# Causal attention with 16 heads: every eighth zero-mask product is split between VectorE and GpSimd, with a ScalarE copy of the scores for GpSimd

## The chip, the cores and the metric

The kernel runs on one core of a Trainium2 chip. The metric is the device time of one execution in microseconds (us). The engines are TensorE (PE; its weight loads are listed as PEld), VectorE (DVE), ScalarE (ACT), GpSimd (POOL) and SyncE (SP). Each works through its own list of instructions in order, and they meet at semaphores.

## The reference

The whole reference is two transformer-like layers over 4096 tokens of width 256. The change touches only the attention of the first layer, with 16 heads of width 16:

```
q, k = rope(q), rope(k)                       # 16 heads, 4096 tokens, width 16
scores = einsum('bhsd,bhtd->bhst', q, k) / 4
scores = scores * tril(ones)
scores = where(scores == 0.0, -inf, scores)
out = einsum('bhst,bhtd->bhsd', softmax(scores), v)
```

A score that is exactly zero gets no weight, whether the causal mask made it so or not. So each exponential has to be multiplied by (score != 0).

## The kernel before

`phase_attend` works on transposed scores: 128 keys lie on the partitions and 512 queries on the free axis. The 16 heads form four groups g of HG = 4 heads. For each group the 4096 queries are cut into eight blocks j of BT = 512 (32 blocks in all). Block j runs over the key tiles kt = 0 .. 4j+3 of 128 keys. One (g, j, kt) is a step, and there are 576. The last four steps of a block meet the diagonal (`diag` = 0 .. 3) and work on the columns from `w0` on: 512, 384, 256 and 128 of them. All others have 512 columns. In the 448 steps off the diagonal `diag` is None.

A step has two units, pair 0 (heads 0 and 1) and pair 1 (heads 2 and 3). Unit u = 2n + pair, of step number n, uses the scores buffer u % 3 of `ps_s`: two PSUM banks, one for each head, three such buffers. A unit goes through three engines:

- TensorE, `score`, L795: two bf16 matmuls of 128x512 into `ps_s`. It first waits until VectorE has done unit u-3, which used the same buffer (semaphore `bank`).
- ScalarE, L847: one exponential of 128x1024 out of `ps_s` into `probs` in SBUF, which has four slots, one for each step.
- VectorE, L874: one `scalar_tensor_tensor` over 128x1024: (score != 0) times the exponential. Its first input is in PSUM, its second and its output are in SBUF.

In diagonal steps GpSimd then cuts the triangle with one `affine_select` over four heads of 128x128 (L887). At last TensorE does `weigh` (L808): for each of the four heads a f32 matmul with the values, which accumulates in `ps_o` (each is listed as two instructions, so eight in a step).

The order on TensorE is written out by hand: for step n it is score(n, pair 1), score(n+1, pair 0), weigh(n-2). So an odd unit (pair 1) is always scored behind a `weigh`, and an even unit right behind an odd one. Once a block, ScalarE also copies the 128x512 result of the block before out of PSUM (L838, in the second diagonal step for j > 0). The key and query transfers are issued by SyncE.

Of the kernel before, what the change touches and what calls it, by code (L numbers as in the profile page):

```python
# [9 lines left out]
ALU = mybir.AluOpType  # L10
ACT = mybir.ActivationFunctionType
# [11 lines left out]
BT = 512  # L23
NB = T // BT
TT = BT // P
NT = T // P
HG = 4
# [91 lines left out]
class Carver:  # L119


    def __init__(self, tensor, at=0):
        self.tensor, self.at = tensor, at
        self.size = tensor.shape[1]
# [509 lines left out]
class Step:  # L634


    def __init__(self, n, g, j, kt):
        self.n, self.g, self.j, self.kt = n, g, j, kt
        self.block = g * NB + j
        self.slot = n % 4  # L640
        self.first = kt == 0
        self.diag = kt - TT * j if kt >= TT * j else None
        self.last = self.diag == TT - 1
        self.w0 = P * self.diag if self.diag else 0

    def unit(self, pair):

        return 2 * self.n + pair

    def masked(self):  # L650

        return self.block * TT + self.diag + 1
# [8 lines left out]
def all_steps():  # L661

    n = 0
    for g in range(NG):
        for j in range(NB):
            for kt in range(TT * (j + 1)):
                yield Step(n, g, j, kt)
                n += 1
# [5 lines left out]
def copied_in(step):  # L674


    if step.diag == (1 if step.j else 2) and step.block:
        return step.block - 1
# [18 lines left out]
def phase_attend(nc, m):  # L697


    with ExitStack() as ctx:  # L700
        own = []

        def sem(name):
            own.append(nc.alloc_semaphore(name="b_" + name))
            return own[-1]
# [4 lines left out]
        a = Carver(m.arena2)  # L710
        probs = a.take(4, HG, BT)
        a = Carver(m.arena, HG * T)
        q_stack = a.take(2, HG, BT, dt=BF16)
        o_raw = a.take(BT)
        recips = a.take(TT, HG)
        o_out = a.take(2, TT, HG, DH)

        ps_s = pb("ps_s", [P, 3, 2, BT])
        ps_o = pb("ps_o", [P, 2, BT])

        scored, exped, bank, probs_free = sem("scored"), sem("exped"), sem("bank_free"), sem("probs_free")
        masked, kload, o_copied = sem("masked"), sem("k_loaded"), sem("o_copied")
        o_turned, o_ready, recip_done = sem("o_turned"), sem("o_ready"), sem("recip_done")
        q_in = [sem("q_in0"), sem("q_in1")]
        o_stored = [sem("o_stored0"), sem("o_stored1")]
        block = ctx.enter_context(nc.Block())
# [52 lines left out]
        @block.tensor  # L779
        def _(pe):  # L780
            pe.wait_ge(m.kload_first, 16 * 8 * (NB - 1))

            def score(step, pair):
                u = step.unit(pair)
                if step.first and pair == 0:
                    pe.wait_ge(q_in[step.block % 2], 128 * (step.block // 2 + 1))
                    if step.block == NB - 1:
                        pe.wait_ge(m.kload_last, 128)
                    if step.j == 0 and step.g > 0:
                        pe.wait_ge(kload, 128 * step.g)  # L790
                if u >= 3:
                    pe.wait_ge(bank, u - 2)
                for h in range(2):
                    head = step.g % 2 * HG + 2 * pair + h
                    last = pe.matmul(ps_s[:, u % 3, h, step.w0:], m.k_stack[:, head, step.kt * P:step.kt * P + P],  # L795
                                     q_stack[:, step.block % 2, 2 * pair + h, step.w0:], start=True, stop=True)
                last.then_inc(scored, 1)

            def weigh(step):
                if step.first and step.block >= 2:  # L800
                    pe.wait_ge(o_ready, step.block - 1)
                if step.diag is None:
                    pe.wait_ge(bank, step.unit(1) + 1)
                else:
                    pe.wait_ge(masked, step.masked())
                for h in range(HG):
                    at = (step.kt * NH + step.g * HG + h) * (DH + 1)
                    last = pe.matmul(ps_o[32 * h:32 * h + 32, step.block % 2, step.w0:], m.values_flat[:, at:at + 32],  # L808
                                     probs[:, step.slot, h, step.w0:], start=step.first, stop=step.last,
                                     tile_position=(0, 32 * h))  # L810
                last.then_inc(probs_free, 1)

            def turn_over(b):
                pe.wait_ge(o_copied, b + 1)
                for t in range(TT):
                    last = pe.transpose(ps_o[:, b % 2, t * P:t * P + P], o_raw[:, t * P:t * P + P], m.ident[:])
                last.then_inc(o_turned, 1)

            with pe.If(bounded(pe) > 0):
                steps = list(all_steps())  # L820
                score(steps[0], 0)
                for step in steps:
                    score(step, 1)
                    if step.n + 1 < len(steps):
                        score(steps[step.n + 1], 0)
                    if step.n >= 2:
                        weigh(steps[step.n - 2])
                    if turned_in(step) is not None:
                        turn_over(turned_in(step))
                weigh(steps[-2])  # L830
                weigh(steps[-1])
                turn_over(BLOCKS - 1)

        @block.scalar
        def _(act):
            def copy_out(b):
                act.wait_ge(probs_free, steps_through(b))
                act.activation(o_raw, ps_o[:, b % 2], ACT.Copy).then_inc(o_copied, 1)  # L838

            with act.If(bounded(act) > 0):  # L840
                for step in all_steps():
                    if step.n >= 4:
                        act.wait_ge(probs_free, step.n - 3)
                    for pair in range(2):
                        u = step.unit(pair)
                        act.wait_ge(scored, u + 1)
                        act.activation(probs[:, step.slot, 2 * pair:2 * pair + 2, step.w0:], ps_s[:, u % 3, :, step.w0:], ACT.Exp,  # L847
                                       scale=1.0 / DH ** 0.5).then_inc(exped, 1)
                    if copied_in(step) is not None:
                        copy_out(copied_in(step))  # L850
                copy_out(BLOCKS - 1)

        @block.vector
        def _(dve):
            def normalise(b):
                dve.wait_ge(o_turned, b + 1)
                turned = ps_o[:, b % 2].rearrange("p (a c) -> p a c", a=TT * HG)
                if b >= 1:
                    dve.wait_ge(o_ready, b)
                dve.reciprocal(recips.rearrange("p t h -> p (t h)"), turned[:, :, DH]).then_inc(recip_done, 1)  # L860
                dve.wait_ge(recip_done, b + 1)
                if b >= 2:
                    dve.wait_ge(o_stored[b % 2], 64 * (b // 2))
                dve.tensor_tensor(o_out[:, b % 2].rearrange("p t h d -> p (t h) d"), turned[:, :, 0:DH],
                                  recips.rearrange("p t (h a) -> p (t h) a", a=1).to_broadcast([P, TT * HG, DH]), ALU.mult)\
                   .then_inc(o_ready, 1)

            with dve.If(bounded(dve) > 0):
                for step in all_steps():
                    for pair in range(2):  # L870
                        u = step.unit(pair)
                        dve.wait_ge(exped, u + 1)
                        p = probs[:, step.slot, 2 * pair:2 * pair + 2, step.w0:]
                        dve.scalar_tensor_tensor(p, ps_s[:, u % 3, :, step.w0:], 0.0, p, ALU.not_equal, ALU.mult).then_inc(bank, 1)  # L874
                    if normalised_in(step) is not None:
                        normalise(normalised_in(step))
                normalise(BLOCKS - 1)

        @block.gpsimd
        def _(pool):  # L880
            with pool.If(bounded(pool) > 0):
                for step in all_steps():
                    if step.diag is not None:

                        pool.wait_ge(bank, step.unit(1) + 1)
                        sq = probs[:, step.slot, :, step.w0:step.w0 + P]
                        pool.affine_select(out=sq, in_=sq, compare_op=ALU.is_ge, fill=0.0, base=0,  # L887
                                           pattern=[[0, HG], [1, P]], channel_multiplier=-1).then_inc(masked, 1)
# [1164 lines left out]
```

## Time and profile before

| | |
|---|---|
| median of three runs | 2300.75 us (2298.0 to 2304.64) |
| the profiled execution | 2298.0 us, of which the span from first to last instruction is 2296.3 us |
| busy over the span | PE 88%, DVE 75%, ACT 60%, POOL 24% |
| mean granted TensorE clock | 0.970 of full speed, 1.00 in most of the attention stage |
| attention stage | from about 189 us to about 1463 us of the span |

Times on the timeline are microseconds from the start of the span. An instruction's row gives its start and its duration. On ScalarE and VectorE the next instruction may begin some 0.1 us before the one ahead of it has ended, so the distance from start to start is what an instruction really takes of its engine when it stands in a queue. The count after x says how many instructions a row merges. A text in square brackets is the idle time ahead of the instruction and what ended it. "Releaser" is the profile's own inference.

### The profile page before, as it was taken

Reading aid. Unit: us, or ns where it says so; the run is one execution under the profiler, and the core shown is the slowest. Engines: PE = TensorE matmul, PEld = TensorE weight load, DVE = VectorE, ACT = ScalarE, POOL = GpSimd, SP = SyncE. Lnnn points to the kernel's source line nnn. Section 1 sums busy time; section 2 is a strip of 40 time slices with the busy share of each in tenths; the row PEclk is TensorE's granted clock in tenths of the full one; section 3 lists DMA queues with packets and bytes.
Section 4 is the critical chain, followed back from the end, with each engine's and each line's share of the span. In section 5 each row is a group of like instructions: output and inputs, shape, how many; then the busy total and the mean of one; then the engine's idle time right before and its main releaser. Section 6 shows DMA issues by size and latency. Waiting matters only on the chain. (4 is left out here: it accounts for less than half of the span.)

```text
span 2296.3 us, 28755 instructions
## 1 busy us (share of the span) xinstructions
PE 2009.7 (88%) x10349; PEld 807.0 (35%) x10349; DVE 1714.2 (75%) x2280; ACT 1366.9 (60%) x1729; POOL 542.7 (24%) x553
## 2 busy tenths in 40 slices
PE   4986999998999989999989999589886699999997
PEld 3541111111111121111121111256654356777775
DVE  2776999999999999999999999557665543333332
ACT  0675888888888888888888888345554211111110
POOL 1681000000000010000010000026655174323324
PEclk8997999999999999999999999899998899999999
DMA  3463211102111111212530000210000043444441
GB/s 110 155 197 96 42 30 22 30 14 52 21 31 22 30 45 35 38 21 64 163 102 12 13 12 3 80 37 20 18 1 1 7 148 115 113 103 93 110 102 23
DMA packets 124641, 133.85 MB, mean 58 GB/s; under 512 B 35145, under 2 KB 118946, under 8 KB 123808
## 3 DMA queue, kind: packets, MB, share of 16 engines
q1 hardware_dynamic: 109920, 118.09, 19.0%
q0 software_dynamic: 14592, 14.08, 3.5%
q8 instruction: 76, 1.25, 0.2%
q14 instruction: 53, 0.43, 0.1%
HBM read 97.08 MB, written 50.63 MB: 64 GB/s over the span
## 5 line engine op out<-in xcount | busy, mean ns | idle before, releaser
L874 DVE SCALAR_TENSOR_TENSOR arena<-ps_s,arena 128x1024 f32<-128x1024 f32 (+3 forms) x1152 | 1212.7, 1128 | 49.8 <-ACT arena L847 43.5
L847 ACT ACTIVATE arena<-ps_s 128x1024 f32<-128x1024 f32 (+3 forms) x1152 | 1046.0, 952 | 226.1 <-PE ps_s L795 221.5
L795 PE MATMUL ps_s<-arena 128*128 128x512 bf16 (+3 forms) x2304 | 648.0, 368 | 119.0 <-DVE arena L874 56.1
L808 PE MATMUL ps_o<-arena,values 128*32 128x512 f32 (+3 forms) x4608 | 574.8, 571 | 0.4 <-POOL arena L887 0.4
L795 PEld LDWEIGHTS ps_s<-arena 128*128 128x128 bf16 x2304 | 136.3, 97 | 792.7 <-DVE arena L874 770.0
L887 POOL TENSOR_SCALAR_AFFINE_SELECT arena<-arena 128x512 f32<-128x512 f32 x128 | 81.6, 637 | 1201.8 <-DVE arena L874 1201.8
L1801 ACT ACTIVATE arena<-g_ps_g 128x320 f32<-128x320 f32 (+1 forms) x96 | 42.2, 439 | 310.8 <-PE g_ps_u L1735 310.8
L1986 POOL DMA_INDIRECT out<-values,slot_ids x80 | 123.4, 1543 | 240.6 <-DVE values L1950 212.3
L1923 DVE TENSOR_TENSOR arena<-g_ps_u,arena 128x320 f32<-128x320 f32 (+1 forms) x96 | 47.2, 492 | 168.3 <-ACT arena L1801 168.3
L808 PEld LDWEIGHTS ps_o<-arena,values 128*32 128x32 f32 x4608 | 90.8, 108 | 225.3 <-issue 207.7
L1228 PE MATMUL t_ps_out<-arena 128*128 128x256 f32 x512 | 124.8, 402 | 19.7 <-DVE arena L1458 8.8
L1735 PE MATMUL g_ps_g<-arena 128*128 128x320 f32 (+1 forms) x384 | 119.7, 434 | 0.6 <-issue 0.6
L1735 PE MATMUL g_ps_u<-arena 128*128 128x320 f32 (+1 forms) x384 | 120.1, 435 | 0.0
L1228 PEld LDWEIGHTS t_ps_out<-arena 128*128 128x128 f32 x512 | 102.3, 203 | 42.3 <-issue 19.9
L1750 PE MATMUL g_ps_d<-arena 128*128 128x256 f32 (+1 forms) x480 | 107.9, 381 | 1.0 <-DVE arena L1923 1.0
L1750 PEld LDWEIGHTS g_ps_d<-arena 128*128 128x128 f32 (+1 forms) x480 | 89.5, 189 | 15.2 <-DVE arena L1923 1.6
L1967 POOL DMA_INDIRECT slots_in_dram<-arena,scatter_at x64 | 70.3, 1099 | 55.0 <-issue 55.0
L1236 PE MATMUL t_ps_turn<-ident,arena 128*128 128x128 f32 x256 | 37.4, 294 | 51.1 <-ACT arena L1122 18.8
L1950 DVE SCALAR_TENSOR_TENSOR values<-g_ps_d,arena,gates 128x256 f32<-128x256 f32 x80 | 35.8, 481 | 61.9 <-PE g_ps_d L1750 61.9
L1735 PEld LDWEIGHTS g_ps_u<-arena 128*128 128x128 f32 (+1 forms) x384 | 69.8, 182 | 34.5 <-issue 0.6
L1735 PEld LDWEIGHTS g_ps_g<-arena 128*128 128x128 f32 (+1 forms) x384 | 69.5, 181 | 33.2 <-issue 1.4
L1325 ACT ACTIVATE arena<-t_ps_turn,mod_cols 128x512 f32<-128x512 f32 x48 | 34.8, 775 | 71.5 <-PE t_ps_turn L1236 71.5
(198 smaller groups left out, 1640.2 us busy)
## 6 DMA issues: line engine op xcount, KB each, us to landing
arena<-parts_dram SPq DMA_DIRECT2D x320, 64.0 KB, 2.3
parts_dram<-arena SPq DMA_DIRECT2D x32, 384.0 KB, 2.9
arena<-parts_dram SPq DMA_DIRECT2D x24, 512.0 KB, 7.0
slots_in_dram<-in_empty_slots SPq DMA_DIRECT2D x10, 1040.0 KB, 25.8
arena<-slots_in_dram SPq DMA_DIRECT2D x16, 650.0 KB, 4.6
arena<-in_L_ffn_w_gate SPq DMA_DIRECT2D x16, 352.0 KB, 3.1
arena<-in_L_ffn_w_up SPq DMA_DIRECT2D x16, 352.0 KB, 3.8
arena<-in_L_attn_x SPq DMA_DIRECT2D x8, 512.0 KB, 3.9
```

Of the source, the lines that this page charges most:

```text
L795: last = pe.matmul(ps_s[:, u % 3, h, step.w0:], m.k_stack[:, head, step.kt * P:step.kt * P + P], q_stack[:, step.block % 2, 2 * pair + h, ...
L808: last = pe.matmul(ps_o[32 * h:32 * h + 32, step.block % 2, step.w0:], m.values_flat[:, at:at + 32], probs[:, step.slot, h, step.w0:], sta ...
L847: act.activation(probs[:, step.slot, 2 * pair:2 * pair + 2, step.w0:], ps_s[:, u % 3, :, step.w0:], ACT.Exp, scale=1.0 / DH ** 0.5).then_i ...
L874: dve.scalar_tensor_tensor(p, ps_s[:, u % 3, :, step.w0:], 0.0, p, ALU.not_equal, ALU.mult).then_inc(bank, 1)
L887: pool.affine_select(out=sq, in_=sq, compare_op=ALU.is_ge, fill=0.0, base=0, pattern=[[0, HG], [1, P]], channel_multiplier=-1).then_inc(ma ...
L1228: last = pe.matmul(ps_out[:, c, t * D:t * D + D], lhs[:, k, at:at + P], w[:, k], start=k == 0, stop=k == KC - 1)
L1735: last = pe.matmul(ps[0:rows_, n % 2, 0:HALF], w[:, s, k, at:at + rows_], inT[:, s, k, half * HALF:half * HALF + HALF], start=k == 0, stop ...
L1750: last = pe.matmul(ps_d[:, (s + i) % 2, at:at + D], hidden_e[0:rows_, s, f, c * P:c * P + P], w_down[0:rows_, s, f], start=f == 0, stop=f ...
L1801: act.activation(silu_e[0:rows_, n % 2], ps_g[0:rows_, n % 2, 0:HALF], ACT.Silu).then_inc(silued, 1)
L1923: dve.tensor_tensor(hidden_e[0:rows_, s, i, half * HALF:half * HALF + HALF], ps_u[0:rows_, n % 2, 0:HALF], silu_e[0:rows_, n % 2], ALU.mul ...
L1967: pool.indirect_dma_start(out=m.slots_in[:, :], out_offset=bass.IndirectOffsetOnAxis(ap=m.scatter_at[:, k, t:t + 1], axis=0), in_=m.h_wide ...
L1986: pool.indirect_dma_start(out=out_rows, out_offset=bass.IndirectOffsetOnAxis(ap=ids[:, s, c:c + 1], axis=0), in_=rows_out[:, s, c], in_off ...
```

## The change

In every step with `diag` None and kt % 4 == 1 (kt = 1, 5, 9, ... 4j-3; j of them in block j, 28 for each group, 112 in all) the last head's product leaves VectorE. VectorE's instruction of pair 1 then covers one head (128x512). ScalarE copies the last head's 128x512 scores out of `ps_s` into `s_copy` in SBUF, behind the exponential of pair 1. GpSimd turns the copy into ones and zeros with a `tensor_scalar`, and multiplies the exponentials by it with a `tensor_tensor`. TensorE waits for the copy (`scores_out`) before it scores pair 0 two steps later (kt % 4 == 3), which uses the same buffer, and for GpSimd's product (`last_masked`) before it weighs the step.

```diff
+        self.shared = self.diag is None and kt % 4 == 1
...
+        return self.g * NB * (NB - 1) // 2 + self.j * (self.j - 1) // 2 + min((self.kt + 2) // 4, self.j)
...
+        s_copy = a.take(BT)
...
                 if u >= 3:
                     pe.wait_ge(bank, u - 2)
+                if pair == 0 and step.kt % 4 == 3 and step.diag is None:
+                    pe.wait_ge(scores_out, step.shares())
...
                 if step.diag is None:
                     pe.wait_ge(bank, step.unit(1) + 1)
+                    if step.shared:
+                        pe.wait_ge(last_masked, step.shares() + 1)
...
+                    if step.shared:
+                        if step.shares():
+                            act.wait_ge(last_masked, step.shares())
+                        act.activation(s_copy, ps_s[:, step.unit(1) % 3, 1], ACT.Copy).then_inc(scores_out, 1)
...
-                        p = probs[:, step.slot, 2 * pair:2 * pair + 2, step.w0:]
-                        dve.scalar_tensor_tensor(p, ps_s[:, u % 3, :, step.w0:], 0.0, p, ALU.not_equal, ALU.mult).then_inc(bank, 1)
+
+                        heads = 1 if step.shared and pair == 1 else 2
+                        p = probs[:, step.slot, 2 * pair:2 * pair + heads, step.w0:]
+                        dve.scalar_tensor_tensor(p, ps_s[:, u % 3, 0:heads, step.w0:], 0.0, p, ALU.not_equal, ALU.mult).then_inc(bank, 1)
...
+                    if step.shared:
+                        pool.wait_ge(scores_out, step.shares() + 1)
+                        pool.wait_ge(exped, step.unit(1) + 1)
+                        pool.tensor_scalar(s_copy, s_copy, 0.0, 0.0, ALU.is_equal, ALU.is_equal).then_inc(kept, 1)
+                        pool.wait_ge(kept, step.shares() + 1)
+                        p = probs[:, step.slot, HG - 1]
+                        pool.tensor_tensor(p, p, s_copy, ALU.mult).then_inc(last_masked, 1)
```

## Rows read from the trace of the kernel before

**Rows 1.** The attention stage: busy us (xcount) of each engine, granted clock, DMA.

```profile
185.00:1465.00 1280.00, 1163.94 (x7040) 239.57 (x7040) 1231.42 (x1216) 1058.17 (x1184) 81.56 (x128) 0.99 0.18 39
```

**Rows 2.** The page's costliest groups: busy us, mean ns, idle before, releaser.

```profile
L874 DVE SCALAR_TENSOR_TENSOR arena<-ps_s,arena 128x1024 f32<-128x1024 f32 (+3 forms) x1152 | 1212.7, 1128 | 49.8 <-ACT arena L847 43.5
L847 ACT ACTIVATE arena<-ps_s 128x1024 f32<-128x1024 f32 (+3 forms) x1152 | 1046.0, 952 | 226.1 <-PE ps_s L795 221.5
...
L887 POOL TENSOR_SCALAR_AFFINE_SELECT arena<-arena 128x512 f32<-128x512 f32 x128 | 81.6, 637 | 1201.8 <-DVE arena L874 1201.8
```

**Rows 3.** VectorE's masking by shape, all of the span.

```profile
L874 DVE SCALAR_TENSOR_TENSOR arena<-ps_s,arena 128x1024 f32<-128x1024 f32 x960 | 1092.3, 1217 | 22.4 <-ACT arena L847 19.2
...
L874 DVE SCALAR_TENSOR_TENSOR arena<-ps_s,arena 128x512 f32<-128x512 f32 x64 | 43.6, 686 | 3.1
```

**Rows 4.** Timeline of ACT, DVE, PEld around kt = 5 of one block (start, us).

```profile
924.91 1.02 ACT L847 ACTIVATE arena<-ps_s 128x1024 f32<-128x1024 f32 x1 [0.32 <-PE ps_s L795]
...
925.83 1.02 ACT L847 ACTIVATE arena<-ps_s 128x1024 f32<-128x1024 f32 x1
...
927.17 1.02 ACT L847 ACTIVATE arena<-ps_s 128x1024 f32<-128x1024 f32 x1 [0.33 <-PE ps_s L795]
...
925.99 1.22 DVE L874 SCALAR_TENSOR_TENSOR arena<-ps_s,arena 128x1024 f32<-128x1024 f32 x1
...
927.12 1.22 DVE L874 SCALAR_TENSOR_TENSOR arena<-ps_s,arena 128x1024 f32<-128x1024 f32 x1
...
926.52 0.11 PEld L795 LDWEIGHTS ps_s<-arena 128*128 128x128 bf16 x2 [0.84 <-DVE arena L874]
927.25 0.11 PEld L795 LDWEIGHTS ps_s<-arena 128*128 128x128 bf16 x2 [0.62 <-DVE arena L874]
927.79 0.16 PEld L808 LDWEIGHTS ps_o<-arena,values 128*32 128x32 f32 x8 [0.42 <-issue]
928.79 0.11 PEld L795 LDWEIGHTS ps_s<-arena 128*128 128x128 bf16 x2 [0.84 <-DVE arena L874]
```

**Rows 5.** Timeline around kt = 1 of the same block.

```profile
914.53 1.93 ACT L847 ACTIVATE arena<-ps_s 128x1024 f32<-128x1024 f32 x2
...
916.65 1.02 ACT L847 ACTIVATE arena<-ps_s 128x1024 f32<-128x1024 f32 x1 [0.18 <-PE ps_s L795]
...
917.72 1.02 ACT L847 ACTIVATE arena<-ps_s 128x1024 f32<-128x1024 f32 x1
...
916.94 1.22 DVE L874 SCALAR_TENSOR_TENSOR arena<-ps_s,arena 128x1024 f32<-128x1024 f32 x1
...
918.07 1.22 DVE L874 SCALAR_TENSOR_TENSOR arena<-ps_s,arena 128x1024 f32<-128x1024 f32 x1
```

**Rows 6.** Timeline of ACT, its copy out of PSUM and the next exponential.

```profile
908.52 0.59 ACT L838 ACTIVATE arena<-ps_o 128x512 f32<-128x512 f32 x1
...
909.00 0.60 ACT L847 ACTIVATE arena<-ps_s 128x512 f32<-128x512 f32 x1
```

**Rows 7.** Timeline where VectorE waited for an exponential.

```profile
912.35 1.02 ACT L847 ACTIVATE arena<-ps_s 128x1024 f32<-128x1024 f32 x1
...
913.40 1.23 DVE L874 SCALAR_TENSOR_TENSOR arena<-ps_s,arena 128x1024 f32<-128x1024 f32 x1
```

**Rows 8.** A GpSimd product with two SBUF inputs: duration ns min/median/max.

```profile
L516 POOL TENSOR_TENSOR arena<-arena x32: 1146/1160/1608, 67.0 to 173.9; 128x512 f32<-128x512 f32 x32
```

**Rows 9.** VectorE lines, some beside GpSimd: duration ns min/median/max, first and last start.

```profile
L471 DVE TENSOR_TENSOR arena<-arena x32: 679/1020/1662, 65.4 to 171.3; 128x512 f32<-128x512 f32 x32
...
L458 DVE TENSOR_TENSOR arena<-ps_p,arena x16: 658/692/693, 62.9 to 167.2; 128x512 f32<-128x512 f32 x16
...
L874 DVE SCALAR_TENSOR_TENSOR arena<-ps_s,arena x1152: 414/1215/1226, 191.5 to 1459.4; 128x1024 f32<-128x1024 f32 x160, 128x768 f32<-128x768 f32 x20, 128x256 f32<-128x256 f32 x12
```

**Rows 10.** Timeline at kt = 1 of a block j = 1.

```profile
837.00 1.03 ACT L847 ACTIVATE arena<-ps_s 128x1024 f32<-128x1024 f32 x1
...
839.13 1.22 DVE L874 SCALAR_TENSOR_TENSOR arena<-ps_s,arena 128x1024 f32<-128x1024 f32 x1
```

More of the change, by code:

```diff
@@ L644, in __init__, with shares @@
         self.w0 = P * self.diag if self.diag else 0
+        self.shared = self.diag is None and kt % 4 == 1
     def unit(self, pair):
         return 2 * self.n + pair
+    def shares(self):
+        return self.g * NB * (NB - 1) // 2 + self.j * (self.j - 1) // 2 + min((self.kt + 2) // 4, self.j)
     def masked(self):
@@ L723, in phase_attend @@
         o_turned, o_ready, recip_done = sem("o_turned"), sem("o_ready"), sem("recip_done")
+        scores_out, kept, last_masked = sem("scores_out"), sem("kept"), sem("last_masked")
         q_in = [sem("q_in0"), sem("q_in1")]
```

## The prediction

> **What bounds the kernel now.** I read the page first, then the stage in one window, then the lines by shape, and then the timeline, which decides. The slices of the page put the attention between 189 and 1463 us. In that window VectorE is busy 1231 of 1280 us, TensorE 1164, ScalarE 1058, and GpSimd 82 [rows 1]. Nearly all of VectorE's time is L874: 1152 instructions, 1212.7 us, with only 49.8 us of idle time ahead of them; ScalarE waits 226 us for scores [rows 2]. That invites one to say "VectorE is the bound, take work off it". Busy shares don't say how far ahead of VectorE the others stand, though, and this is what counts when ScalarE is to do more.
>
> So the reader should follow one ordinary step off the diagonal [rows 4]. Let 0 be the start of the multiplication of pair 1 of step kt = 5, unit u1 (925.99). The multiplication of u2 starts at 1.13 (927.12), though each lasts 1.22: 1.13 is what one takes of VectorE. The exponential of u1 started at -1.08 (924.91), that of u2 at -0.16 (925.83), so one takes 0.92 of ScalarE. It ended at 0.86 (925.83 + 1.02), 0.27 before VectorE took it up. In the place where VectorE plainly waits, it starts 0.03 after the exponential's end (912.35 + 1.02, then 913.40) [rows 7], so of the 0.27 some 0.24 is spare. That is all the lead that ScalarE has ahead of an even unit.
>
> Why has it no more, though it is idle 0.32 in a step? Because of the loop through TensorE: VectorE frees u1's buffer at 1.22, TensorE scores u4 0.04 later (927.25) and `weigh` follows 0.54 behind (927.79), the odd unit u5 is scored 1.00 after that (928.79), its exponential starts 0.65 after its score (as 926.52 to 927.17), lasts 1.02, and 0.03 later u5 can be multiplied. The sum is 1.22 + 0.04 + 0.54 + 1.00 + 0.65 + 1.02 + 0.03 = 4.50, and VectorE needs 4 x 1.13 = 4.52 for the four units. **Two limits lie within 0.02 us**: VectorE's own rate, and this loop. There are two such loops, one through u1, u5, u9 and one through u3, u7, u11.
>
> **The change, part by part.** There are 112 shared steps: 28 with kt = 1, and 84 with kt = 5 or more.
>
> *VectorE's shorter product.* 128x1024 lasts 1217 ns, 128x512 686 ns [rows 3]: 0.53 saved each time, 59 us in all, if the next exponential were there.
>
> *ScalarE's copy.* The change has no row of its own here; the nearest is L838, a copy of 128x512 out of PSUM, 0.59 long, with the next exponential 0.48 after its start [rows 6]. As low bound I take the per-column part of ScalarE's time alone: (1.02 - 0.60) for 512 columns [rows 4, 6], 0.42. As high bound the whole 0.59, plus 0.05 for the extra semaphore instructions, an estimate from the hand-over gaps of 0.03 and 0.04 above, rounded up. I take 0.48: same shape, same source, same engine.
>
> *Timetable of a shared step with kt >= 5.* The copy starts at -1.08 + 0.92 = -0.16, and the exponential of u2 at -0.16 + 0.48 = 0.32 (before: -0.16). It ends at 1.34, and VectorE takes it up at 1.37. Before, it was 1.13. VectorE has been ready since 0.69 - 0.09 = 0.60. So the 0.53 saved turns into waiting, and u2 is **0.24 later than before**. What is late next? The exponential of u3 moves from 1.18 to 0.32 + 0.92 = 1.24 and ends at 2.26, in time for u3 at 1.37 + 1.13 = 2.50. The score of u4 needs VectorE's end of u1 (0.69), the copy's end (0.43) and TensorE's own turn, all before its old place at 1.26; u5 comes early too. But from u2 on VectorE runs at its 1.13, so nothing wins the 0.24 back. The next shared unit, u9, is scored behind VectorE's end of u5 and a `weigh`, and u5 is 0.24 later as well. So the exponential of u9 again stands only 1.08 ahead of VectorE, and the loss repeats. 84 x 0.24 = **+20.4 us** (0.18 and 0.40 at the bounds of the copy: +15 and +34).
>
> *Shared steps with kt = 1.* Behind the short diagonal steps ScalarE is further ahead. With 0 at 916.94, the exponential of u1 starts at -1.50 (914.53 + 1.93 - 1.02 = 915.44), that of u2 at -0.29 (916.65) and of u3 at 0.78 (917.72) [rows 5]. Now the copy starts at -0.58, u2's exponential at -0.10 and ends at 0.92, and u2 is multiplied at 0.95 instead of 1.13 (918.07): 0.18 won. u3 keeps it (its exponential, from 0.82 to 1.84, is in time for 2.08). This holds in 25 of the 28. In the blocks j = 1 of groups 1 to 3 the lead is 2.13 (837.00, 839.13) [rows 10]. There u2 gains the full 0.53, but u3's exponential isn't moved by the change (0.78 to 1.80), so u3 starts at 1.83 instead of 2.26, 0.43 won at most; I take 1.0 us for the three. 25 x 0.18 + 1.0 = **-5.5 us** (0 to -8 at the bounds).
>
> *GpSimd's two instructions.* Nearest rows: 0.64 for 128x512 with one input (L887) [rows 2] and 1.16 for a product with two [rows 8]. Neither shows a comparison; I take 0.64 and keep 1.16 as high bound. From the copy's end at 0.43 the chain ends at about 0.43 + 0.64 + 1.16 + 0.2 of hand-overs = 2.4 (2.9 at the high bound). `weigh` of this step comes behind the score of u6, which waits for the end of u3: 2.50 + 1.22 + 0.04 + 0.54 = 4.3. Cost 0, with 1.4 to 1.9 us of cover. Queued behind that wait are the score of u7 and every one after it. Each 1 us beyond the cover would put 112 us on the path.
>
> *The waits.* `scores_out` on TensorE is served at 0.43, before VectorE's 0.69: 0. ScalarE's wait for `last_masked` is for the shared step four steps back: 0.
>
> The sum is 20.4 - 5.5 = +15 us. On the profiled execution's 2298.0 us that makes 2313; that one was the fastest of three, 2.75 below the median, so against the median of 2300.75 us I predict **2316 us**.
>
> **The rivals.** (A) *The exponential isn't held up, VectorE's saving counts.* It needs a copy that costs under 0.24 beside the exponentials, or a lead of 0.24 more. Half of what an exponential takes is 0.46, so the rows speak against it. Even so the loop through u3 and u7 has no shared unit in it: 2 x 4.50 for eight units against 9.05 now allows 0.03 to 0.05 a step, 84 x 0.04 = 3, with 5.5 of kt = 1: about 2292 us. Only if the loop too were slack would all 59 us come: 2242. (B) *Half of the loss*: a lead that grows, for instance because u5 and the exponentials behind it run early. With 0.12 in place of 0.24 it is 10 - 5.5 = +4.6: 2305, no change that can be measured. (C) *GpSimd and VectorE hold each other up.* L471, both inputs in SBUF, is 0.68 at its best and 1.13 in the mean over its 32, beside GpSimd's work; L458, with an input in PSUM and in the same stretch, stays at 0.66 to 0.69; and L874 never passes 1.23, with 128 GpSimd instructions among its 1152 [rows 9]. L874 has one input in PSUM, so the second pattern should hold. If not, two multiplications each shared step take 0.45 more: 112 x 0.9 = 101 us, 2417. If they shut each other out wholly, it is 112 x 1.8 = 202 us.
>
> By the Trainium skill (SBUF — State Buffer, section "Who interferes with whom") a VectorE instruction with two SBUF inputs contends with a GpSimd instruction that reads SBUF, and whoever comes second is blocked wholly. Applied to L874 that would be the 202 us of (C). The same section exempts an instruction with at most one SBUF input outside the two-port modes, and on that the trace agrees (0.69 at most for L458, against 1.66 for L471).
>
> (D) *GpSimd is late.* A comparison of 3.2 us instead of 0.64 would overrun the cover by 0.7: +78, 2394. No row comes near it.
>
> **How the numbers follow.** Measured against no change, 0.3% is 7 us. The mechanism above 0.79: at its bounds the sum runs from +15 - 8 = +7 to +34 - 0 = +34, so 2308 to 2335. (A) 0.06, (B) 0.09, (C) 0.03, (D) 0.03. The range, 2304 to 2335, takes in most of (B); it leaves out (A), (C), (D) and a little of the rest. Slower by over 0.3% are the mechanism but for its lowest end, (C) and (D): 0.82. Same are (B) and that end: 0.12. Faster is (A): 0.06.
>
> **What the profile after would show.** Right: L874 in about 112 instructions of 0.69 more and as many of 1.22 fewer; a copy line on ScalarE of x112 at about 0.59; idle time of VectorE behind ScalarE's L847 up from 44 us by 84 x (1.37 - 0.60) = 65 and 28 x 0.35 = 10 to some 115 to 120; busy VectorE down by some 60; even units after a shared one of kt >= 5 start 1.37 after it, and of kt = 1 0.95. Wrong: VectorE idle no more than before; L874's 1217 ns grown (C); TensorE's `weigh` waiting for GpSimd off the diagonal (D); or the even unit behind a shared one at 1.13 or earlier (A, B). What would break the forecast most easily is the cost of the copy beside the exponentials, since every 0.01 us of it is worth 1 us.

## The result

| | before | changed |
|---|---|---|
| median | 2301.31 us (4 runs, 2298.0 to 2304.64) | 2318.09 us (4 runs, 2317.34 to 2320.04) |
| span of the profiled execution | 2296.3 us | 2315.5 us |

The ratio is 1.0075, with a 95% interval of 1.0056 to 1.0092: the change makes the kernel slower by 16.8 us, where +15 was forecast. VectorE has less to do and ScalarE stays below it, and yet the time is longer.

The page of the changed kernel, its costliest groups, answers to [rows 2]:

```profile
L892 DVE SCALAR_TENSOR_TENSOR arena<-ps_s,arena 128x1024 f32<-128x1024 f32 (+3 forms) x1152 | 1163.1, 1076 | 114.5 <-ACT arena L859 108.1
L859 ACT ACTIVATE arena<-ps_s 128x1024 f32<-128x1024 f32 (+3 forms) x1152 | 1053.3, 959 | 192.7 <-PE ps_s L805 173.9
...
L820 PE MATMUL ps_o<-arena,values 128*32 128x512 f32 (+3 forms) x4608 | 573.5, 570 | 0.4 <-POOL arena L912 0.4
L904 POOL TENSOR_SCALAR arena<-arena 128x512 f32<-128x512 f32 x112 | 215.0, 1919 | 611.1 <-ACT arena L864 611.1
...
L907 POOL TENSOR_TENSOR arena<-arena 128x512 f32<-128x512 f32 x112 | 142.6, 1274 | 9.3
```

VectorE's masking is busy 49.6 us less, but its idle time behind the exponentials has gone from 43.5 to 108.1 us. TensorE's `weigh` waits for nothing but the triangle cut (L912), as before. Same kernel, lines by shape (answers to [rows 3], and gives the copy's row that was missing before):

```profile
L892 DVE SCALAR_TENSOR_TENSOR arena<-ps_s,arena 128x1024 f32<-128x1024 f32 x848 | 976.1, 1217 | 87.2 <-ACT arena L859 83.9
...
L892 DVE SCALAR_TENSOR_TENSOR arena<-ps_s,arena 128x512 f32<-128x512 f32 x176 | 119.8, 683 | 3.1
...
L864 ACT ACTIVATE arena<-ps_s 128x512 f32<-128x512 f32 x112 | 67.0, 598 | 0.0
```

112 more products are short now (176 against 64 in [rows 3]), and 112 fewer are long (848 against 960). The timeline shows where the idle time sits. This is the shared step kt = 5 of the same block as [rows 4], with the next shared product at the end (ScalarE, then VectorE, then GpSimd, then TensorE's weight loads):

```profile
931.46 1.02 ACT L859 ACTIVATE arena<-ps_s 128x1024 f32<-128x1024 f32 x1 [0.32 <-PE ps_s L805]
...
932.38 0.59 ACT L864 ACTIVATE arena<-ps_s 128x512 f32<-128x512 f32 x1
...
932.86 1.95 ACT L859 ACTIVATE arena<-ps_s 128x1024 f32<-128x1024 f32 x2
...
932.54 0.68 DVE L892 SCALAR_TENSOR_TENSOR arena<-ps_s,arena 128x512 f32<-128x512 f32 x1
...
933.92 1.23 DVE L892 SCALAR_TENSOR_TENSOR arena<-ps_s,arena 128x1024 f32<-128x1024 f32 x1 [0.70 <-ACT arena L859]
...
935.07 1.22 DVE L892 SCALAR_TENSOR_TENSOR arena<-ps_s,arena 128x1024 f32<-128x1024 f32 x1
...
941.85 0.68 DVE L892 SCALAR_TENSOR_TENSOR arena<-ps_s,arena 128x512 f32<-128x512 f32 x1
...
933.06 1.92 POOL L904 TENSOR_SCALAR arena<-arena 128x512 f32<-128x512 f32 x1 [6.04 <-ACT arena L864]
935.06 1.27 POOL L907 TENSOR_TENSOR arena<-arena 128x512 f32<-128x512 f32 x1
...
936.33 0.11 PEld L805 LDWEIGHTS ps_s<-arena 128*128 128x128 bf16 x2 [1.02 <-DVE arena L892]
936.87 0.16 PEld L820 LDWEIGHTS ps_o<-arena,values 128*32 128x32 f32 x8 [0.42 <-issue]
```

With 0 at the short product's start (932.54), the exponential of u1 starts at -1.08 as before, the copy at -0.16, the exponential of u2 at 0.32, and VectorE takes u2 up at 1.38 instead of 1.13, after 0.70 of idle time. From one shared product to the next it is 941.85 - 932.54 = 9.31 us, where eight units took 2 x 4.52 = 9.05. All 60 such distances in this trace lie between 9.30 and 9.32. And at kt = 1 of this block, answering to [rows 5]:

```profile
923.52 1.06 ACT L859 ACTIVATE arena<-ps_s 128x1024 f32<-128x1024 f32 x1
...
923.65 0.68 DVE L892 SCALAR_TENSOR_TENSOR arena<-ps_s,arena 128x512 f32<-128x512 f32 x1
...
924.61 1.22 DVE L892 SCALAR_TENSOR_TENSOR arena<-ps_s,arena 128x1024 f32<-128x1024 f32 x1 [0.28 <-ACT arena L859]
```

There the even unit follows at 0.96 instead of 1.13, and the next shared product stands 932.54 - 923.65 = 8.89 behind, 0.16 less than 9.05.

### The profile page after: what moved, and what is told of

It is laid out like the page before. It is cut to its first block and busy times, and to the rows that moved or that the text cites. A ratio compares the mean times of both kernels' runs of the same rounds, so it can differ in the third digit from the quotient of the medians.

```text
span 2315.5 us, 29427 instructions
## 1 busy us (share of the span) xinstructions
PE 2003.0 (87%) x10349; PEld 816.3 (35%) x10349; DVE 1665.2 (72%) x2280; ACT 1414.9 (61%) x1841; POOL 899.9 (39%) x777
## 5 line engine op out<-in xcount | busy, mean ns | idle before, releaser
L892 DVE SCALAR_TENSOR_TENSOR arena<-ps_s,arena 128x1024 f32<-128x1024 f32 (+3 forms) x1152 | 1163.1, 1076 | 114.5 <-ACT arena L859 108.1
L805 PE MATMUL ps_s<-arena 128*128 128x512 bf16 (+3 forms) x2304 | 632.6, 367 | 145.1 <-DVE arena L892 98.8
L904 POOL TENSOR_SCALAR arena<-arena 128x512 f32<-128x512 f32 x112 | 215.0, 1919 | 611.1 <-ACT arena L864 611.1
L805 PEld LDWEIGHTS ps_s<-arena 128*128 128x128 bf16 x2304 | 143.1, 97 | 801.6 <-DVE arena L892 761.1
L912 POOL TENSOR_SCALAR_AFFINE_SELECT arena<-arena 128x512 f32<-128x512 f32 x128 | 81.2, 635 | 239.2 <-DVE arena L892 239.2
L907 POOL TENSOR_TENSOR arena<-arena 128x512 f32<-128x512 f32 x112 | 142.6, 1274 | 9.3
```

The lines of the kernel that those rows point to most:

```text
L892: dve.scalar_tensor_tensor(p, ps_s[:, u % 3, 0:heads, step.w0:], 0.0, p, ALU.not_equal, ALU.mult).then_inc(bank, 1)
L904: pool.tensor_scalar(s_copy, s_copy, 0.0, 0.0, ALU.is_equal, ALU.is_equal).then_inc(kept, 1)
L907: pool.tensor_tensor(p, p, s_copy, ALU.mult).then_inc(last_masked, 1)
```

## Experiments

The theory (lead and loops): a copy on ScalarE delays the next even unit by what exceeds its spare lead of 0.24 us, VectorE never wins that back, and what VectorE saves is worth next to nothing, since the loops through TensorE, 4.51 us for four units, stand right behind VectorE's 4.52. The rivals: VectorE's time is the bound, so that its saving counts; and GpSimd's work costs the time, by holding VectorE up or by being late for `weigh`. Each kernel was timed in turn with the kernel before, and each ratio is to that.

**Only the shorter product.** From the changed kernel:

```diff
-                if pair == 0 and step.kt % 4 == 3 and step.diag is None:
-                    pe.wait_ge(scores_out, step.shares())
...
-                    if step.shared:
-                        pe.wait_ge(last_masked, step.shares() + 1)
...
-                        act.activation(s_copy, ps_s[:, step.unit(1) % 3, 1], ACT.Copy).then_inc(scores_out, 1)
...
-                        pool.tensor_scalar(s_copy, s_copy, 0.0, 0.0, ALU.is_equal, ALU.is_equal).then_inc(kept, 1)
-                        pool.wait_ge(kept, step.shares() + 1)
-                        p = probs[:, step.slot, HG - 1]
-                        pool.tensor_tensor(p, p, s_copy, ALU.mult).then_inc(last_masked, 1)
```

> Leaves out the test for exact zeros of one head in the 112 shared steps: VectorE's product is half as long there, and there is no copy, no GpSimd work and no wait for them. By the theory of the two loops through TensorE: a loop without a shared unit takes 4.51 us for four units against 4.52, so the 84 steps with kt >= 5 give 0.03 us each, 2.5 in all; in the 28 with kt = 1 the exponential of u3 allows 0.43 each, 12. Together -14 or -15: about 2287 us. By the rival that VectorE's own rate is the bound: 112 x 0.53 = 59 less, 2242 us.

Measured: 2289.55 us, ratio 0.9945 (0.9932 to 0.9958), some 13 us less and not 59. A second look at the same kernel, on another chip, had this expectation:

> A second look at the kernel that only has the shorter product (the test for exact zeros of one head left out in 112 steps), on the same chip: 2287 to 2290 us again.

It gave 2286.19 us in its one run, 0.8 below that range. The kernel before had a median of 2302.8 us on the same chip, so this is 16.6 less, but one run gives no interval. The timeline of the first look, at kt = 5 (VectorE) and with the exponential of u3, and below it u1 and u2 at kt = 1 of the same block:

```profile
920.59 0.68 DVE L884 SCALAR_TENSOR_TENSOR arena<-ps_s,arena 128x512 f32<-128x512 f32 x1
...
921.49 1.22 DVE L884 SCALAR_TENSOR_TENSOR arena<-ps_s,arena 128x1024 f32<-128x1024 f32 x1 [0.21 <-ACT arena L855]
...
922.83 1.22 DVE L884 SCALAR_TENSOR_TENSOR arena<-ps_s,arena 128x1024 f32<-128x1024 f32 x1
...
929.63 0.68 DVE L884 SCALAR_TENSOR_TENSOR arena<-ps_s,arena 128x512 f32<-128x512 f32 x1
...
921.78 1.02 ACT L855 ACTIVATE arena<-ps_s 128x1024 f32<-128x1024 f32 x1 [0.32 <-PE ps_s L803]
...
911.90 0.68 DVE L884 SCALAR_TENSOR_TENSOR arena<-ps_s,arena 128x512 f32<-128x512 f32 x1
...
912.66 1.23 DVE L884 SCALAR_TENSOR_TENSOR arena<-ps_s,arena 128x1024 f32<-128x1024 f32 x1
```

u2 comes at 0.90, 0.23 early, but u3 at 2.24, only 0.02 early: its exponential had to wait for TensorE. Eight units take 929.63 - 920.59 = 9.04. So with no cost at all on ScalarE and GpSimd, an ordinary shared step gives 0.01 to 0.02 us for 0.53 of VectorE's work. That is the second limit: 84 x 0.015 is little over 1 us. What gain there is comes from kt = 1. There the next shared product follows 920.59 - 911.90 = 8.69 after the one shown, 0.36 less than 9.05, and 28 x 0.36 = 10 us. The expectation had 12 us for this part and 2.5 for the other.

**The changed kernel without GpSimd's work** (the copy and the short product stay):

```diff
-                    if step.shared:
-                        pe.wait_ge(last_masked, step.shares() + 1)
...
-                            act.wait_ge(last_masked, step.shares())
+                            act.wait_ge(scores_out, step.shares())
...
-                        pool.tensor_scalar(s_copy, s_copy, 0.0, 0.0, ALU.is_equal, ALU.is_equal).then_inc(kept, 1)
...
-                        pool.tensor_tensor(p, p, s_copy, ALU.mult).then_inc(last_masked, 1)
```

> Leaves out the test for exact zeros of one head in the 112 shared steps: the changed kernel with ScalarE's copy and VectorE's half product, but without GpSimd's two instructions and TensorE's wait for them. If the copy alone costs the time: as the changed kernel, 2318 us, within 2. If GpSimd's work held VectorE up or was late for TensorE (its chain ended only 0.53 us ahead of the weigh): faster than the changed kernel, by 5 us or more.

Measured: ratio 1.0075 (1.006 to 1.0091), the changed kernel's own. The median is 2321.07 us, 3 above 2318 where "within 2" was expected, but the six runs fall apart into four near 2321 and two near 2312 (2311.4 to 2322.01). The two have a mean granted clock of 0.970 and 0.971, the four 0.968 or 0.969; where that comes from isn't shown. The profiled execution is one of the two near 2312, and even in it the attention is as in the changed kernel: u2 comes 1.38 behind a shared unit with kt >= 5, and from the first masking product to the last it takes 1282.7 us against 1283.1. So GpSimd's 358 us of new work cost nothing there. VectorE's idle time behind the exponentials is the changed kernel's too:

```profile
L890 DVE SCALAR_TENSOR_TENSOR arena<-ps_s,arena 128x1024 f32<-128x1024 f32 (+3 forms) x1152 | 1162.6, 1074 | 114.8 <-ACT arena L857 108.4
```

**Only the copy**, in the kernel before. So that it doesn't read the bank that VectorE reads, it goes from SBUF to SBUF, which makes it 627 ns long instead of 598:

```diff
+                    if step.shared:
+                        if copies[0]:
+                            act.wait_ge(scores_out, copies[0])
+                        act.activation(s_copy[:, 0:512], m.values_flat[:, 0:512], ACT.Copy).then_inc(scores_out, 1)
+                        copies[0] += 1
```

> The kernel before with nothing changed but a ScalarE copy of 128x512 (SBUF to SBUF) behind the exponential of pair 1 in the 112 shared steps. VectorE keeps its full product. By the lead theory: 84 steps lose what the changed kernel loses in each, 0.26 (+22); in the 28 with kt = 1 the spare lead swallows the copy (0). About 2323 us: only 5 worse than the changed kernel, since VectorE's saved 59 us is worth only what kt = 1 can use. If VectorE's saving is really used in the changed kernel, this one should be some 60 us worse than that: about 2375. If the copy is free beside the exponentials: 2301.

> As the kernel with the 128x512 copy alone, but 128x128: by the slope of ScalarE's rows it takes about 0.16 us of ScalarE instead of 0.48. By the lead theory there is a threshold at 0.24 us, and 0.16 is under it: no loss, 2301 us. If every ScalarE nanosecond counted: 112 x 0.16 = 18 us, 2319.

Measured with 512 columns: 2326.68 us, ratio 1.0107 (1.0093 to 1.0122), +25 us. The copy is 0.03 longer than the one from PSUM, and 84 x 0.03 = 2.5 is most of the 3.7 us that it lies above the 2323 of the theory; the rest is within the noise. At kt = 5 of the block of [rows 4] VectorE takes 1.41 from odd to even unit with the full product, and the changed kernel takes 1.38 with the half one; the longer copy makes the 0.03. At kt = 1 of that block it takes 1.13 as before, so there the spare lead swallows the copy, as expected. The two products at kt = 5:

```profile
936.12 1.21 DVE L883 SCALAR_TENSOR_TENSOR arena<-ps_s,arena 128x1024 f32<-128x1024 f32 x1
...
937.53 1.23 DVE L883 SCALAR_TENSOR_TENSOR arena<-ps_s,arena 128x1024 f32<-128x1024 f32 x1 [0.20 <-ACT arena L851]
```

Measured with 128 columns: 2304.9 us, ratio 1.0012 (1.0004 to 1.0021), 2.8 us where 0 was expected and 18 by the rival. The copy took 0.20 us of ScalarE (the distance from its start to the next exponential's in the 84 steps with kt >= 5) and not the 0.16 expected, but this is still under 0.24, and the trace has no step that it delays: u2 follows at 1.13 and the next shared product at 9.05, as before. The page of that kernel has 47.0 us of VectorE's waits for exponentials, against 43.5 before and 59.0 with 512 columns.

```profile
L883 DVE SCALAR_TENSOR_TENSOR arena<-ps_s,arena 128x1024 f32<-128x1024 f32 (+3 forms) x1152 | 1212.5, 1123 | 53.3 <-ACT arena L851 47.0
```

In the profiled executions the attention is 2.9 us longer than before (193.0 to 1463.8 against 191.5 to 1459.4), and nearly all of that lies in the shortest blocks, j = 0 and j = 1. There, apart from the start of the stage, where both traces have it, TensorE's granted clock falls to 0.50, its lower level of 1.2 GHz: three times in this trace and once in the one before (at 521.6). One of the three, with TensorE busy for only 0.71 of the 2 us ahead of it (three windows of `--windows`, columns as in [rows 1]; then the `weigh` at that place, which took 1.06 us elsewhere):

```profile
1158.00:1160.00 2.00, 0.71 (x6) 0.11 (x2) 2.00 (x3) 1.33 (x2) 0.00 (x0) 0.99 0.39 98
1160.00:1162.00 2.00, 1.97 (x10) 0.34 (x10) 2.00 (x2) 1.40 (x2) 0.00 (x0) 0.50 0.08 16
1162.00:1164.00 2.00, 2.00 (x12) 0.38 (x4) 1.44 (x2) 0.45 (x2) 0.00 (x0) 0.66 0.00 0
...
1160.99 1.93 PE L811 MATMUL ps_o<-arena,values 128*32 128x512 f32 x8
```

VectorE then waited for an exponential for 1.35 us. Such falls come without any copy too, as in the first trace of the shorter product alone (two), while the trace with the 512-column copy has none in these blocks; whether the small copy makes them likelier isn't shown.

**The shared head from the even unit.** Same work on each engine, but the copy stands behind the exponential of pair 0, where ScalarE idled 0.32:

```diff
-                if pair == 0 and step.kt % 4 == 3 and step.diag is None:
+                if pair == 1 and step.kt % 4 == 2 and step.diag is None:
...
-                        act.activation(s_copy, ps_s[:, step.unit(1) % 3, 1], ACT.Copy).then_inc(scores_out, 1)
...
+                        if step.shared and pair == 0:
...
+                            act.activation(s_copy, ps_s[:, u % 3, 1], ACT.Copy).then_inc(scores_out, 1)
...
-                        heads = 1 if step.shared and pair == 1 else 2
+                        heads = 1 if step.shared and pair == 0 else 2
...
-                        p = probs[:, step.slot, HG - 1]
+                        p = probs[:, step.slot, 1]
```

> The changed kernel with the shared head taken from pair 0 (even unit) instead of pair 1: the copy follows the exponential of the even unit, where ScalarE idled 0.32 us in a step. By the lead theory the copy then fills that gap but for 0.16 us less VectorE's tie: the next odd exponential starts at 0.76 + 0.48 = 1.24 instead of 1.19, so the odd unit is multiplied about 0.04 later: 84 x 0.04 = +3.5, and some us won at kt = 1. About 2298 to 2304 us, 15 to 20 better than the changed kernel with the same work on every engine. If the mere amount of ScalarE's work counts: 2318 as the changed kernel.

Measured: 2305.38 us, ratio 1.0009 (0.9997 to 1.002): no difference from the kernel before, which had 2303.71 us beside it, and by the ratios some 15 us better than the changed kernel. At kt = 5 (ScalarE: the exponential of the even unit, the copy, the exponential of u1; VectorE: the short product of the even unit, the product of u1, and the next short one):

```profile
923.56 1.02 ACT L859 ACTIVATE arena<-ps_s 128x1024 f32<-128x1024 f32 x1
924.47 0.61 ACT L864 ACTIVATE arena<-ps_s 128x512 f32<-128x512 f32 x1
...
924.94 1.05 ACT L859 ACTIVATE arena<-ps_s 128x1024 f32<-128x1024 f32 x1
...
924.85 0.68 DVE L892 SCALAR_TENSOR_TENSOR arena<-ps_s,arena 128x512 f32<-128x512 f32 x1
...
926.02 1.23 DVE L892 SCALAR_TENSOR_TENSOR arena<-ps_s,arena 128x1024 f32<-128x1024 f32 x1 [0.49 <-ACT arena L859]
...
933.95 0.68 DVE L892 SCALAR_TENSOR_TENSOR arena<-ps_s,arena 128x512 f32<-128x512 f32 x1
```

The product of u1 starts 926.02 - 924.85 = 1.17 behind the even unit's instead of 1.13, the 0.04 of the expectation, and eight units take 9.10 instead of 9.05. So it is the place of the copy that costs, not the amount of ScalarE's work. The edit moves the short product too, to the even unit, and no run moves the copy alone; but by the rows a full product there would have let VectorE go on at 1.13, before the 1.17 that the exponential allows.

**Twice as many shared steps**, all odd kt:

```diff
-        self.shared = self.diag is None and kt % 4 == 1
+        self.shared = self.diag is None and kt % 2 == 1
...
-                if pair == 0 and step.kt % 4 == 3 and step.diag is None:
-                    pe.wait_ge(scores_out, step.shares())
+                if pair == 0 and step.n >= 2 and SHARED[step.n - 2]:
+                    pe.wait_ge(scores_out, SHARES[step.n - 1])
```

> The changed kernel with twice as many shared steps: every odd kt off the diagonal, 224. If each copy costs 0.26 us as in the changed kernel: about 84 + 112 steps at that, +50: 2350. By the loop theory the cost isn't per copy: only the loop through u3, which then has no shared unit and no delayed one in its way, sets the rate (4.51 us for four units, the same as before within 0.02), provided that GpSimd's 3.3 us fit into the 4.5 between two copies: about 2290 to 2300 us. If GpSimd's chain doesn't fit it is late for the weigh: above 2330.

Measured: 2293.91 us, ratio 0.9958 (0.9944 to 0.9972). Twice the copies, and the loss is gone. The timeline at kt = 5 (the copy, the exponential of u2; then the products of u1, of u2 and of the shared unit eight units on):

```profile
922.28 0.59 ACT L869 ACTIVATE arena<-ps_s 128x512 f32<-128x512 f32 x1
922.76 1.03 ACT L864 ACTIVATE arena<-ps_s 128x1024 f32<-128x1024 f32 x1
...
922.72 0.68 DVE L897 SCALAR_TENSOR_TENSOR arena<-ps_s,arena 128x512 f32<-128x512 f32 x1
...
923.82 1.22 DVE L897 SCALAR_TENSOR_TENSOR arena<-ps_s,arena 128x1024 f32<-128x1024 f32 x1 [0.42 <-ACT arena L864]
...
931.75 0.68 DVE L897 SCALAR_TENSOR_TENSOR arena<-ps_s,arena 128x512 f32<-128x512 f32 x1
```

Every unit of the loop u1, u5, u9 is now short, so this loop has 0.53 to spare, its exponentials run further ahead (the copy starts at 922.28 - 922.72 = -0.44 instead of -0.16), and u2 follows at 1.10. The loop u3, u7 without any short unit sets the rate: eight units take 931.75 - 922.72 = 9.03, twice the old 4.51 or 4.52.

**The loop opened.** `weigh` of an ordinary step is cut by columns into two halves, one behind each score:

```diff
-            def weigh(step):
+            def weigh(step, half=0):
...
+                whole = step.first or step.diag is not None
+                if half == 1 and whole:
+                    return
+                c0, c1 = (step.w0, BT) if whole else (half * BT // 2, half * BT // 2 + BT // 2)
...
-                last.then_inc(probs_free, 1)
+                if whole or half == 1:
+                    last.then_inc(probs_free, 1)
...
                     score(step, 1)
+                    if step.n >= 3:
+                        weigh(steps[step.n - 3], 1)
```

It was put into the kernel before, into the changed one, and into the one with twice the shared steps:

> The kernel before with the weigh of each step off the diagonal (but for kt = 0) split by columns into two halves of 256, one behind each score, so that the loop of a unit through TensorE has one score and no whole weigh in it. TensorE then takes 2 x (0.54 + 0.57) = 2.22 us a step instead of 1.98, against VectorE's 2.26: no change, 2301 us, VectorE bound, with exponentials further ahead. If TensorE can't keep that up: slower.

> The changed kernel with the same two halves. With the loops slack, VectorE's saving counts until TensorE is the bound at 2.22 us a step: up to 0.15 us for each of the 112 shared steps and more at kt = 1: 2280 to 2290 us, faster than both kernels. If the loop isn't what ties the exponentials to VectorE: 2318 as the changed kernel.

> The halves of the weigh together with sharing in every second step (224 of 448). In the kernel with halves and 112 shared steps eight units took 8.91 us against 9.05 before. If TensorE at 2 x (0.54 + 0.57) = 2.22 us a step is what is left as the bound, eight units take 8.87 at least, so only 0.04 more in each of 84, 3 to 6 us in all: 2280 to 2283. If VectorE's time were still the bound: another 0.53 less for each of the 112 steps added, 2226. If GpSimd's chain is late for the first half of the weigh (it had 0.5 us to spare): above 2290.

| | whole `weigh` | in halves |
|---|---|---|
| kernel before | 1 | 1.0005 (0.9996 to 1.0014), 2305.01 us |
| changed, 112 shared steps | 1.0075 (1.0056 to 1.0092), 2318.09 us | 0.9927 (0.9913 to 0.994), 2285.74 us |
| 224 shared steps | 0.9958 (0.9944 to 0.9972), 2293.91 us | **0.991 (0.9896 to 0.9923), 2280.34 us** |

Alone the halves are worth nothing: VectorE is the other limit, and it is untouched. Under the changed kernel they are worth 1.5% of the time and turn its loss into a gain. No run has them with the shorter product alone. The timeline of the changed kernel with halves, at kt = 5 (copy, exponential of u2, products of u1 and u2, and the next shared product):

```profile
914.03 0.59 ACT L873 ACTIVATE arena<-ps_s 128x512 f32<-128x512 f32 x1
...
914.51 1.03 ACT L868 ACTIVATE arena<-ps_s 128x1024 f32<-128x1024 f32 x1
...
914.59 0.68 DVE L901 SCALAR_TENSOR_TENSOR arena<-ps_s,arena 128x512 f32<-128x512 f32 x1
...
915.57 1.23 DVE L901 SCALAR_TENSOR_TENSOR arena<-ps_s,arena 128x1024 f32<-128x1024 f32 x1 [0.30 <-ACT arena L868]
...
923.50 0.68 DVE L901 SCALAR_TENSOR_TENSOR arena<-ps_s,arena 128x512 f32<-128x512 f32 x1
```

The copy now starts 0.56 ahead of the product of u1, not 0.16, and u2 follows at 0.98 instead of 1.38. Eight units take 923.50 - 914.59 = 8.91, so an ordinary shared step gives 0.14 of VectorE's 0.53, where at most 0.15 was expected. The last kernel is the best of all, faster than the kernel before by 0.9%. There the third limit shows, at kt = 5 and behind it (TensorE's weight loads of score and half `weigh` in turn, then two shared products eight units apart):

```profile
911.02 0.11 PEld L810 LDWEIGHTS ps_s<-arena 128*128 128x128 bf16 x2 [0.43 <-DVE arena L906]
911.56 0.16 PEld L830 LDWEIGHTS ps_o<-arena,values 128*32 128x32 f32 x8 [0.42 <-issue]
912.13 0.11 PEld L810 LDWEIGHTS ps_s<-arena 128*128 128x128 bf16 x2 [0.41 <-issue]
...
910.88 0.68 DVE L906 SCALAR_TENSOR_TENSOR arena<-ps_s,arena 128x512 f32<-128x512 f32 x1
...
919.74 0.68 DVE L906 SCALAR_TENSOR_TENSOR arena<-ps_s,arena 128x512 f32<-128x512 f32 x1
```

A score follows the last one at 1.11 (0.54 and 0.57), 2.22 a step as expected, and eight units take 8.86. TensorE's own work is now the limit, and twice the shared steps bring only 0.05 more in eight units, where 0.04 was expected.

## Why the prediction was right

- **The lead of 0.24 us behind an odd unit.** Right: u2 at 1.38 where 1.37 was worked out. The copy's own row (598 ns, the next exponential 0.48 after its start) is that of L838.
- **The loss isn't won back.** Right: 9.31 - 9.05 = 0.26 for a step with kt >= 5, forecast 0.24; 84 x 0.26 = 21.8 us where 20.4 was forecast. The difference is that u2 comes at 1.38 and not 1.37, and that u3 starts 1.14 behind u2, not 1.13 (1.14 in the mean over these steps; 935.07 - 933.92 in the rows).
- **kt = 1 wins a little.** Right, and a little too large: 0.16 instead of 0.18. 25 x 0.16 = 4 us. The three blocks j = 1 give about 1.2 (eight units from 8.78 down to 8.37 in each), so 5.2 where 5.5 was forecast, and the sum is 21.8 - 4.0 - 1.2 = 16.6 us. That 16.8 were measured is closer than the times can tell, which scatter by several us for the same kernel; in the two profiled executions the attention grew by 15.2 us (from 191.5 to 1459.4 before, from 191.2 to 1474.4 changed), and only the one before has the fall of the clock at 521.6 in it. The rows of single steps carry the argument, not this agreement.
- **VectorE's saving is worth nothing beyond that, because of the loop.** Right: with the shorter product alone 13 us came and not 59, nearly all of it from kt = 1, and with the loop opened the changed kernel became faster than the one before.
- **GpSimd at no cost.** Right in the result, wrong in a term. The comparison took 1.92 us, not 0.64, and more than the high bound of 1.16; the product took 1.27 instead of 1.16. The chain ended at 935.06 + 1.27 = 936.33, and `weigh` began at 936.87. So the cover was 0.54 us and not 1.4 to 1.9. The chain ended 3.79 behind the product of u1, not 2.4 or at most 2.9, so that it still cost nothing was in part luck. The nearest row, a triangle cut, was no measure for a comparison, and the bounds should have said so.
- **No contention (rival C).** Right: L892 isn't longer than L874 was (1217 ns), and without GpSimd's work the ratio is the same 1.0075, with u2 at the same 1.38.
- **The signs to look for.** VectorE's idle time behind the exponentials is 108 us, forecast 115 to 120; its busy time fell by 49.6 and not 60. Both are the same slip: an instruction with idle time behind it counts with its full 0.69, where I had put 0.60. 84 x (1.38 - 0.69) + 28 x (0.96 - 0.69) = 66, and 43.5 + 66 = 109.

## What to carry to other kernels

Before work is moved off the busiest engine, measure in the timeline how far ahead of it the others stand at that very place, and sum up the longest loop of buffer hand-overs: where lead is 0.24 us and the loop within 0.02 of the engine's own rate, a relief of 0.53 buys 0.01 to 0.02 and a helper's 0.48 costs 0.26 each time. Where two limits lie together, each cure alone shows little (the halves of `weigh` 1.0005, the shorter product 0.01 to 0.02 us in an ordinary step) and the two together show more (0.14 us, and 0.9927 with the copy's cost paid); so a failed change is worth trying again once the other limit is gone. Where the added work stands in an engine's order can matter more than its amount: the same copy, with the same amount of work beside it, made the kernel 17 us slower behind one exponential and made no difference behind the other.

## What the runs showed of the hardware

- GpSimd's `tensor_scalar` with two `is_equal` on 128x512 f32 took 1919 ns, three times its triangle cut over as many elements (635 ns in the same trace).
- VectorE's product with one input in PSUM kept its 1217 ns beside more than five times as much GpSimd work as before (439 us of the stage against 82).
- A VectorE product that starts after idle time took 1.23 instead of 1.22 us, and behind the delayed u2 of the changed kernel the next one followed 1.14 after its start, not 1.13.
- TensorE's granted clock fell to 0.50 three times in the short blocks of the kernel with the 128-column copy. At one of them, TensorE had been busy for 0.71 of 2 us before, and a `weigh` took 1.93 us instead of 1.06.
